# First node stage of a four-layer graph network: the gate multiplication moves from GpSimd to ScalarE, and GpSimd's angle steps move between two additions

## The reference, cut to what matters

```python
x = _layernorm(x + _L0_gnn_ref(x, node_vec1, edge_attr_4, edge_attr_8, ...), axis=-1)
x = _layernorm(x + _L1_gnn_ref(...), axis=-1)
x = _layernorm(x + _L2_gnn_ref(...), axis=-1)
x = _layernorm(x + _L3_gnn_ref(...), axis=-1)
```

```python
conv = ...   # 160 columns, linear in the summed messages, times node_attr
sc = ...     # 160 columns, linear in x, times node_attr
angle = 0.1 * (ms @ W3) * node_attr * (1.0 / np.sqrt(MUL0 + MUL1))
cos, sin = (jnp.cos(angle), jnp.sin(angle))
return cos * sc + sin * conv
```

## Time and profile before

| | value |
|---|---|
| median of 3 runs | 4107.62 us |
| the profiled execution, own time | 4101.09 us |
| its span | 4098.9 us |
| busy in the span: PE / DVE / POOL / ACT | 86% / 68% / 61% / 55% |
| node stage of the first layer, first gate to last normalisation | 698.3 to 1207.9 us |

### The profile page before, as it was taken

The page is one execution under the profiler, slowest core; times in us unless marked ns, Lnnn a source line. Parts: engine busy times, 40 slices in busy tenths (PEclk is TensorE's granted clock), DMA queues, the critical chain, the costliest instruction groups (busy, mean ns, idle before and its releaser), DMA issues.

```text
span 4098.9 us, 104392 instructions
## 1 busy us (share of the span) xinstructions
PE 3520.8 (86%) x26652; PEld 3264.2 (80%) x26652; DVE 2803.2 (68%) x10450; ACT 2255.1 (55%) x6189; POOL 2500.3 (61%) x3168
## 2 busy tenths in 40 slices
PE   0599998666659999989979999989989999977776
PEld 0599997656649999977769999977779999976665
DVE  0477775888876666668876666678866666656666
ACT  0244443555544444457765555567766666658888
POOL 0377776777766777756657777600036666657776
PEclk9999999777769999999999999999999999989999
DMA  9522222556642222259862222178842222136665
GB/s 390 179 82 63 61 56 86 187 196 200 202 137 59 58 57 55 48 192 300 298 200 64 62 61 57 39 271 300 298 130 56 54 52 50 44 109 223 222 226 193
DMA packets 423009, 575.44 MB, mean 140 GB/s; under 512 B 218250, under 2 KB 241802, under 8 KB 419144
## 3 DMA queue, kind: packets, MB, share of 16 engines
q1 hardware_dynamic: 280746, 293.10, 24.3%
q10 hardware_dynamic: 60512, 166.57, 10.3%
q0 software_dynamic: 81648, 114.57, 9.8%
HBM read 359.42 MB, written 233.39 MB: 145 GB/s over the span
## 4 chain that ended last, share of the span: by engine, by line
PE 60%; ACT 15%; POOL 8%; issue 8%; ACTq 3%; DMA 2%; DVE 2%; another core or an unknown queue 2%; POOLq 1%; SPq 1%; DVEq 0%
PE bank L734 17%; PE bank L767 12%; ACT arena L986 9%; PE bank L777 5%; PE bank L787 3%; PE bank L724 3%; PE bank L790 3%; PE bank L741 3%; PE bank L782 3%; POOL arena L632 3%; ACT same_all L974 3%; PE bank L759 3%; ACTq L959 2%; POOL arena L636 2%; ACT nT L963 2%
## 5 line engine op out<-in xcount | busy, mean ns | idle before, releaser
L545 POOL DMA_INDIRECT aggregates<-arena,meta x784 | 792.0, 1010 | 436.5 <-issue 252.5
L986 ACT ACTIVATE arena<-arena,shift,rstd 128x160 f32<-128x160 f32 x1600 | 699.3, 514 | 180.3 <-DVE shift L1251 177.6
L734 PE MATMUL bank<-same_all,msg 128*98 (+1 forms) x6272 | 750.7, 273 | 0.0
L533 POOL DMA_INDIRECT xg<-x_after,meta x588 | 584.7, 994 | 252.7 <-issue 249.7
L734 PEld LDWEIGHTS bank<-same_all,msg 128*98 128x98 f32 x6272 | 708.0, 165 | 0.1
L903 ACT ACTIVATE w<-bank 1x162 f32<-1x162 f32 (+1 forms) x784 | 257.9, 329 | 738.2 <-PE bank L767 736.5
L767 PE MATMUL bank<-w,arena 98*128 98x32 f32 (+1 forms) x4704 | 626.8, 270 | 0.0
L835 PEld LDWEIGHTS bank<-sc_cols,nT 128*128 128x128 f32 x2400 | 358.8, 220 | 288.7 <-issue 287.3
L767 PEld LDWEIGHTS bank<-w,arena 98*128 98x128 f32 x4704 | 588.6, 192 | 0.0
L835 PE MATMUL bank<-sc_cols,nT 128*128 128x128 f32 (+1 forms) x2400 | 371.3, 306 | 178.0 <-ACT nT L963 157.6
L1317 DVE BATCH_NORM_STATS2 stats<-arena 128x6 f32<-128x160 f32 x1600 | 455.5, 314 | 42.2 <-DVE arena L1310 5.8
(11 more groups left out here) (153 smaller groups left out, 7359.5 us busy)
## 6 DMA issues: line engine op xcount, KB each, us to landing
arena<-aggregates SPq DMA_DIRECT2D x400, 324.0 KB, 4.0
x_after<-arena ACTq DMA_DIRECT2D x300, 320.0 KB
arena<-x_after SPq DMA_DIRECT2D x300, 320.0 KB
aggregates<-same_all ACTq DMA_DIRECT2D x4, 8100.0 KB, 72.3
arena<-nodes SPq DMA_DIRECT2D x100, 320.0 KB
out<-arena ACTq DMA_DIRECT2D x100, 320.0 KB
same_all<-sorted_dst SPq DMA_DIRECT2D x7, 1792.0 KB, 6.6
aggregates<-arena,meta POOLq DMA_INDIRECT x784, 2.3
```

The lines of the kernel that those rows point to most:

```text
L533: gp.indirect_dma_start(xg[:, k % XGR, 4 + t * F:4 + (t + 1) * F], None, xtab[l], at).then_inc(gathered[k], 16)
L545: gp.indirect_dma_start(agg, at, tot[:, kk % TRING, t, 0:AW], None, bounds_check=NP - 1, oob_is_err=False).then_inc(spread[kk], 16)
L734: last = nc.tensor.matmul(bank[5 + t][0:MR, c * P:(c + 1) * P], msg[:, k2, t, c, :], same_all[:, bass.ds(here[t], P)], start=True, stop=True)
L986: last = nc.scalar.activation(row, row, ACT.Identity, bias=shift[:, kk, t:t + 1], scale=rstd[:, kk, t:t + 1])
```

## The change

For the first layer, (1) POOL no longer multiplies the aggregates by gate 0: the 128x640 multiplication becomes four ScalarE activations (Copy with a per-partition scale, 128x160 each, in place), put behind the copy to `nT` and ahead of the normalisation of block b-4. They wait for `gates_ready` and the aggregates, and the last signals `gated`. (2) POOL's `angles(b+2)` no longer stands in `make_gates(b)` but behind `gate_and_add(b)`, so between the additions of b and b+1. The place of `sines(b+2)` on ScalarE is unchanged.

```diff
@@ make_gates (POOL)
                         gp.tensor_tensor(g0, pair_of(waves, k)[:, :, 0], a0, ALU.mult)
                         gp.tensor_tensor(g1, pair_of(waves, k)[:, :, 1], a0, ALU.mult).then_inc(gates_ready, 2)
-                        if within(b, 0, NBLK - 2):
-                            angles(b + 2, (k + 2) % NRING, turn + (k + 2) // NRING)
                         return
@@ gate_and_add (POOL)
                     row = an[:, k, :, 2:AW]
                     x = xn[:, k].rearrange("p (t c) -> p t c", t=BT)
-                    gp.tensor_tensor(row, row, gates[:, k, :, 0:1].to_broadcast([P, BT, F]), ALU.mult).then_inc(gated, 1)
                     gp.wait_ge(gated, b + 1)
@@ node_moves (POOL)
                     if l == 0:
                         gate_and_add(b, k, turn)
+                        if k % 2 == 0 and within(b, 0, NBLK - 2):
+                            angles(b + 2, (k + 2) % NRING, turn + (k + 2) // NRING)
@@ node_copies (ACT)
                         if l == 0 and isinstance(b, int) and b == 0:
                             sines(b, k)
+                    if l == 0 and within(b, 0, NBLK):
+                        act.wait_ge(gates_ready, b + 1)
+                        act.wait_ge(a_in[k], node_slot(l, k, turn) * 16)
+                        alone(act, passed["act"])
+                        for j in range(BT):
+                            row = an[:, k, j, 2:AW]
+                            last = nc.scalar.activation(row, row, ACT.Copy, scale=gates[:, k, j, 0:1])
+                        last.then_inc(gated, 1)
```

## The result

The changed kernel takes 4238.82 us (median of 4 runs, 4231.94 to 4240.55) against 4106.51 for the kernel before in the same comparison: **ratio 1.0318, 95% interval 1.0301 to 1.0336, +132 us**. The forecast was slower, 4227 in a range of 4180 to 4285. Run again later beside other kernels it took 4232.91, ratio 1.0315 (1.0297 to 1.0332).

What follows compares the result with a forecast made beforehand. POOL's unbroken sequence, 9.83 us per pair, was taken as the bound. The new ACT-POOL loop of 12.50 adds 2.67 times 49, +131, or +119 with the ends; on the median 4107.6 that gives 4227, range 4180 to 4285.

Steps and rivals of the forecast that it cites:

- What bounded the kernel: First stage: POOL's multiplications, additions, gates and angles follow one another without stopping, 9.83 us per pair of blocks.
- part 3: ACT and POOL order: add(b) waits for gate(b), angles for add(b), sines for angles, gate(b+1) for sines; 12.50 us per pair.
- The cover of the normalisation of b-4: On ACT, its 1.75 us runs beside POOL's addition and angles, costing nothing while the 5.4 us there cover it.
- The sum: Steps from gate(b) to gate(b+2) total 12.50 us per pair against 9.83: +2.67, times 49 is +131; with the ends +119.
- The price of the copy: ACT's gate copies priced like L974, 0.401 us each from PSUM: four end after 1.25, next instruction starts after 1.10.
- The rule that I weighed and left out of the sum: ACT reading SBUF has a fixed 224 cycles against 172 from PSUM: 0.043 us more per copy, some 17 us in total.
- My second route: Price of ACT's copy from SBUF: L986 (about 0.51 us) less a bias pointer's cost, 0.108, gives 0.40.
- The ends: Stage's start and end: gate(0) earlier -3.5, first two pairs about -2.4, last pair +1.2, DVE's tail -7.6 us.
- The signs: Profile after: pair every 12.5 us, some 3.8 us ACT idle before sines, POOL waiting for copies, DVE about two thirds busy.
- (b): Rival, faster: each engine does only its own work, ACT deciding at 8.6 us per pair, if sines never wait; 4049, 4 in 100.

Runs made afterwards that it cites:

- Experiment 1: The changed kernel with the angles put back into make_gates, gate copies still on ACT: 4850.13 us against 4890.97 for the kernel before, ratio 0.991.
- 3: The changed kernel with ACT's sines of the next pair one block later, behind the odd block's normalisation: 4846.80 us, ratio 0.9891.
- 2: The kernel before with only the angles moved between the two blocks' additions, POOL still multiplying: 4897.62 us, ratio 1.002.
- 4: The changed kernel with four extra scaled copies on ACT in even blocks, between normalisation and sines: 5036.40 us against 4890.97, ratio 1.0285.
- Experiment 8: The changed kernel with four extra copies on ACT in odd blocks, read from PSUM, ahead of the nT copy: 4289.74 us, ratio 1.0453.
- experiment 10: The kernel of Experiment 1 run again, against the kernel before: 4053.78 us, ratio 0.9871.
- 5: The changed kernel with four extra scaled copies on ACT in odd blocks, behind the normalisation and ahead of the store: 4267.26 us, ratio 1.04.
- 6: The kernel of Experiment 1 with POOL multiplying the fourth of each block's four rows again: 4052.89 us, ratio 0.9875.
- 11: The kernel of 6 run again: 4053.75 us.
- 9: The kernel of Experiment 1 with the first stage's stores issued one block later: 4119.23 us, ratio 1.0035.

## Why the prediction was right, point by point

- **What bounded the kernel**: POOL's unbroken sequence. Experiment 1 confirms it: with the multiplications gone and the loop open, the pair falls from 9.83 to 8.9.
- **The loop** (part 3): shown. Breaking it at the angles (1) or at the sines (3) takes all of the loss back, with every copy still on ACT. Neither moving the angles without the copies (2) nor moving the copies without the angles (1) costs anything like it.
- **The cover of the normalisation of b-4**: predicted to cost nothing, and 4 shows that even 1.28 us more there cost nothing. ACT's idle before the sines was predicted at 3.8; it is 3.65.
- **The sum**, term by term on the pair above, measured (predicted): gate(b) 1.38 (1.25); signal 0.20 (0.25); add 1.37 (1.38); angles 3.48 (3.46); to ACT 0.25 (0.32); sines 0.61 (0.59); store issue 0.46 (0.43); nT 0.60 (0.60); gate(b+1) 1.28 (1.10); normalisation 1.75 (1.75) and gap 0.76 (0.77); nT 0.60 (0.60). Together 12.74 against 12.50. The mis-sized terms are the two copies', +0.31. The 0.06 that I had added to each of the two signals for the loop was not there, which gives 0.12 back, and the other terms are 0.05 over. Over the stage, from gate(0) to gate(98), the growth is (1323.18 - 704.07) - 481.75 = 137.4 us against 128.6 (131 - 2.4). The steady pairs at 12.71 add 10; the shorter pairs at both ends (11.24, 11.30 and 12.39 for the first three) give some of it back.
- **The price of the copy**: I took L974's, and it was too low because L974 reads PSUM. Experiment 8 shows the source as the difference: 393 ns in the median from PSUM, 421 from SBUF in the same profile, and 1.12 against 1.27 for four. The rule that I weighed and left out of the sum, the Trainium skill's "VectorE: DVE Perf Modes", section on the TRN2 errata, fits better than my price. Its 52 cycles are an estimated 0.043 us per copy. A gate copy added 0.045 more to the rate than my price (1.28 - 1.10 = 0.18 for four), and 0.038 more than a copy from PSUM in the profile of experiment 8 (1.27 - 1.12 = 0.15 for four); by its own duration a copy differs by 0.023 to 0.028 only. My second route, subtracting a bias pointer's cost from L986, assumed that this cost is the same in both operations, and gave 0.40 where 0.418 was measured.
- **The ends**: gate(0) starts 0.51 behind the start of the first gates (704.07 - 703.56), where it was 4.09, so -3.6 (predicted -3.5); the last pair takes 7.20 (predicted 6.9), so +1.5 (+1.2); the tail behind the last addition fell from 18.0 to 11.4, so -6.7 (predicted -7.6). The stage as a whole: 137.4 - 3.6 + 1.5 - 6.7 = +128.6, where the sum had 119. That is 10 of the 12 us from 4227 to 4239. The two profiled spans differ by 139.9; what is over in that comparison lies outside the stage, 5.3 before it and 6.0 behind it, and is not traced here.
- **The signs**: POOL waits for ACT's copies and ACT for POOL's angles, as said. The view of the chain shows nothing for this stretch after the change, so that the engines take turns is read from the timelines and from experiments 1 and 3. One sign was off: DVE was to be busy two thirds of the time and works 308.41 of 590 us, 52%. The 8.33 us per pair that I took for its work held waits, and 6.6 are left. The sum used them only as covered, so the time doesn't depend on it.
- **The rivals**: (b), 4049 if every engine had only its own work to do, is near what experiment 10 gives (4053.78) once the loop is open: -51 us where -59 was forecast, as the pair takes 8.9 and not 8.6. Its condition was the one named: the change as made doesn't meet it. DVE got time back as it says there: L1246 of the earlier trace rows, 1422 ns in the median, is L1253 after the change. What held it before was not tried by itself.

```profile
L1253 DVE TENSOR_SCALAR newton<-var x50: 156/160/182, 719.1 to 1334.8; 128x8 int32<-128x8 int32 x50
```

## What to carry to other kernels

When work moves from one engine to another, write down both engines' program orders and follow each signal until it comes back to where it started. The loop through two queues cost the sum of its steps here, 12.7 us per pair, with its engines busy 62% and 40% of the time. One call moved on either engine took the loss back: with the angles moved (10), +132 us became -51; with the sines moved (3), the ratio was 0.989. Before adding work to a place with idle time, ask what ends that idle time: work on the covered side was free (4), the same work on the other side was not (5).

## What the runs showed beyond that

- A scaled copy of 128x160 on ACT costs 0.023 to 0.028 us more from SBUF than from PSUM by its own duration (5, 8), and 0.04 more by the rate of four in a row (8).
- Work put behind an instruction whose signal a store awaits hides part of that store's gap: four copies worth 1.28 raised the pair by 0.8 only (5).
- Giving work back to POOL relieved ACT and gained nothing (6, 11); DVE's result then came late for ACT. What makes it late was not tried.
- Issuing stores a block later in a ring of eight slots cost 65 us, through SP's queue (9).
